# Linear attention with a tree layer: another order of fills, masking on VectorE, low parts on GpSimd

## The reference

```
xn = layernorm(x)
Q = elu(xn @ Wq + bq) + 1;  K = elu(xn @ Wk + bk) + 1;  V = xn @ Wv + bv     # 16 heads of 64
for each token i:  KV += k_i v_i^T;  Ks += k_i
                   o_i = (q_i KV) / (q_i . Ks + 1e-6)
attention = o @ Wo + bo
gate = sigmoid(xn @ Wq2.T @ routers.T)           # 255 nodes of a binary tree of depth 8
leaf = product of the branch probabilities       # 256 leaves
tree = (leaf @ leaf_values) @ Wout.T + Wout_b
out = x + attention + tree
```

## Time and profile before

| | |
|---|---|
| median of three runs | 1221.74 us |
| profiled execution | 1219.74 us, span 1218.0 us |
| PE busy | 1161.8 us, 95% of the span |
| VectorE, ScalarE, GpSimd busy | 836.1, 681.0, 804.3 us |
| granted PE clock, mean | 0.997 of full speed |
| transfers | 84.46 MB in the main queue |

### The profile page before, as it was taken

The page is one execution under the profiler, slowest core; times in us unless marked ns, Lnnn a source line. Parts: engine busy times, 40 slices in busy tenths (PEclk is TensorE's granted clock), DMA queues, the critical chain, the costliest instruction groups (busy, mean ns, idle before and its releaser), DMA issues.

```text
span 1218.0 us, 48108 instructions
## 1 busy us (share of the span) xinstructions
PE 1161.8 (95%) x21233; PEld 996.0 (82%) x21233; DVE 836.1 (69%) x2186; ACT 681.0 (56%) x990; POOL 804.3 (66%) x951
## 2 busy tenths in 40 slices
PE   5899999999999999999999999999999999999986
PEld 4789788887878879778897888878788797888866
DVE  4775875858677585876858667585876758767482
ACT  3563674737557374673737547374673746647371
POOL 3586667667666676766667676676666667676571
PEclk9999999999999999999999999999999999999998
DMA  7143532525344252533524435252452625335251
GB/s 233 20 80 52 86 68 54 91 52 89 60 65 90 45 97 50 89 63 55 93 49 90 58 62 98 45 89 54 84 68 57 94 45 89 63 57 77 55 71 36
DMA packets 271298, 87.54 MB, mean 72 GB/s; under 512 B 250721, under 2 KB 269424, under 8 KB 271088
## 3 DMA queue, kind: packets, MB, share of 16 engines
q1 hardware_dynamic: 271088, 84.46, 39.0%
HBM read 14.43 MB, written 8.39 MB: 19 GB/s over the span
## 4 chain that ended last, share of the span: by engine, by line
PE 63%; DVE 18%; ACT 6%; DMA 5%; issue 4%; POOL 3%; SPq 1%; POOLq 0%; ACTq 0%; DVEq 0%
PE w_pair L811 17%; PE s_pair L811 11%; PE s_pair L826 9%; PE o_pair L826 9%; PE s_pair L893 5%; PE o_pair L947 4%; DVE snaps L732 4%; DVE qT L659 3%; PE o_pair L933 3%; DVE oT L697 3%; DVE v_aug L668 3%; DVE xn L645 2%; DMA k_turned<-k_planes 2%; PE kv_pair L906 2%; ACT ex L522 2%
## 5 line engine op out<-in xcount | busy, mean ns | idle before, releaser
L406 POOL TENSOR_SCALAR_AFFINE_SELECT aT<-aT 64x512 f32<-64x512 f32 x256 | 171.7, 671 | 264.6 <-ACT aT L562 254.9
L562 ACT ACTIVATE aT<-s_pair 128x512 f32<-128x512 f32 x128 | 76.5, 598 | 382.6 <-PE s_pair L893 382.6
L811 PE MATMUL w_pair<-xnT,wk 128*128 128x512 f32 x768 | 212.1, 411 | 2.2 <-ACT k_tok L535 2.2
L811 PE MATMUL s_pair<-xnT,wq 128*128 128x512 f32 x756 | 201.1, 401 | 0.6 <-DVE o_tok L709 0.3
L732 DVE TENSOR_TENSOR snaps<-kv_pair,snaps 128x65 f32<-128x65 f32 x768 | 173.4, 226 | 26.4
L467 POOL COPY k_tok<-k_turned 128x1024 uint16<-128x1024 uint16 x126 | 171.4, 1361 | 22.7 <-POOL ffn_tok L459 14.6
L811 PE MATMUL w_pair<-wv,xnT 128*128 128x512 f32 x654 | 170.0, 395 | 0.0
L525 ACT ACTIVATE ex<-ex 128x512 f32<-128x512 f32 x256 | 161.9, 633 | 8.1
L449 POOL COPY k_planes<-kT 128x1024 uint16<-128x1024 uint16 x126 | 132.7, 1053 | 49.2 <-issue 26.5
L811 PEld LDWEIGHTS w_pair<-xnT,wk 128*128 128x128 f32 x768 | 134.3, 188 | 34.4 <-ACT k_tok L535 2.7
L811 PEld LDWEIGHTS s_pair<-xnT,wq 128*128 128x128 f32 x756 | 135.1, 188 | 27.0 <-DVE o_tok L709 2.4
(11 more groups left out here) (117 smaller groups left out, 2076.6 us busy)
## 6 DMA issues: line engine op xcount, KB each, us to landing
x_in<-in_L_attn_x_dram SPq DMA_DIRECT2D x16, 256.0 KB, 3.1
x_in<-in_L_attn_x_dram SPq DMA_DIRECT2D x32, 128.0 KB, 3.2
out_dram<-y_buf SPq DMA_DIRECT2D x32, 128.0 KB, 1.7
out_dram<-y_buf SPq DMA_DIRECT2D x64, 64.0 KB, 2.3
k_turned<-k_planes SPq DMA_TRANSPOSE x126, 3.2
stage<-in_L_attn_Wv_dram SPq DMA_DIRECT2D x2, 512.0 KB, 7.8
stage<-in_L_attn_Wk_dram SPq DMA_DIRECT2D x2, 512.0 KB, 10.0
stage<-in_L_attn_Wq_dram SPq DMA_DIRECT2D x2, 512.0 KB, 12.2
```

What stands on the lines that cost most here:

```text
L406: pool.affine_select(out=part, in_=part, compare_op=ALU.is_ge, fill=0.0, base=0, pattern=[[0, 2 * CH], [1, D]], channel_multiplier=-1).the ...
L811: last = pe.matmul(dst, l, r, start=i == 0, stop=i == len(steps) - 1)
```

## The change

The order of fills is another. V1(0) of a block moves from unit 0 to unit 7 of the block before, the two transposes of the next input to units 0 and 1, V1(3) to the head of unit 2, and the gate fills become tails of units 2 and 6 (in bank W1). Unit 5 has no head. The masks leave ScalarE and GpSimd: VectorE takes the minimum of the scores and a tile `limit`, which holds the largest float where a score is kept and 0 elsewhere (the scores are not negative). In each unit VectorE does the mask, then the carry, then the normalisation. GpSimd takes the low part of the turned outputs, after its key copies. The residual is added in four parts (units 2 and 6), x is loaded and normalised in unit 7, and the inverse deviation is computed between the tree's levels.

```diff
 def unit_fills(g, p, blocks):
     ...
-    if p == 0:
-        head, tail = [("V1", 0, g)], [("V1", 1, g)]
-    if p in (1, 2):
-        tail = [("V1", p + 1, g)]
-        if more:
-            head = [("xT", p - 1, g + 1)]
-    if p in (3, 4):
-        head = [("leaf", p - 3, g)]
-        if more:
-            tail = [("V0", p - 3, g + 1)]
-    if p in (5, 6) and more:
-        head, tail = [("gate", p - 5, g + 1)], [("V0", p - 3, g + 1)]
+    if g == 0 and p < HALF - 1:
+        head, tail = (([("V1", 0, 0)], [("V1", 1, 0)]), ([("xT", 0, 1)], [("V1", 2, 0)]),
+                      ([("V1", 3, 0)], [("xT", 1, 1)]))[p]
+    elif p < 2:
+        head = [("xT", p, g + 1)] if more else []
+        tail = [("V1", p + 1, g)]
+    elif p == 2:
+        head = [("V1", 3, g)]
+        tail = [("gate", 0, g + 1)] if more else []
+    elif p in (3, 4):
+        head = [("leaf", p - 3, g)]
+        tail = [("V0", p - 3, g + 1)] if more else []
+    elif p == 5 and more:
+        head = [("gate", 0, 1)] if g == 0 else []
+        tail = [("V0", 2, g + 1)]
+    elif p == 6 and more:
+        head, tail = [("V0", 3, g + 1)], [("gate", 1, g + 1)]
+    elif p == PAIRS - 1 and more:
+        head = [("V1", 0, g + 1)]
 ...
 # sync: the load of x
+                if p == PAIRS - 1 and g + 2 < BLOCKS:
+                    sp.wait_ge(x_consumed, CH * (g + 1))
+                    load_block(g + 2)
                 if by_dma(n):
                     turn_output(n)
                 if n + 3 < UNITS:
                     turn_keys(n + 3)
-                if p == 2 and g + 2 < BLOCKS:
-                    sp.wait_ge(x_consumed, g + 1)
-                    load_block(g + 2)
 ...
 # gpsimd
+            pool.memset(limit[:, :], LARGEST).then_inc(limit_step, 1)
+            pool.wait_ge(limit_step, 1)
+            for a in range(2):
+                part = limit[a * D:(a + 1) * D]
+                pool.affine_select(out=part, in_=part, compare_op=ALU.is_ge, fill=0.0, base=0,
+                                   pattern=[[1, D]], channel_multiplier=-1).then_inc(limit_step, 1)
 ...
+            def low_of_turned(n):
+                g, p = divmod(n, PAIRS)
+                pool.wait_ge(oT_hi, n + 1)
+                pool.tensor_tensor(oT[:, 1, p], o_full[:, 1, p], oT[:, 0, p].bitcast(F32), ALU.subtract)\
+                    .then_inc(o_low, 1)
+                pool.wait_ge(o_low, units_by_dma(n))
 ...
             for n in range(UNITS):
                 g, p = divmod(n, PAIRS)
-                if p == 0 and g + 1 < BLOCKS:
-                    inverse_deviation(g + 1)
-                    pool.wait_ge(rstd_ready, 2 * g + 4)
-                if n + 1 < UNITS:
-                    mask(n + 1)
 ...
                 if n + 3 < UNITS:
                     take_apart(n + 3)
-                if p == 1:
-                    residual(g)
-                    pool.wait_ge(x_consumed, g + 1)
+                if n and by_dma(n - 1):
+                    low_of_turned(n - 1)
+                for c in RESIDUAL_AT.get(p, ()):
+                    residual(g, c)
 ...
                     for l in range(depth):
+                        if l == 4 and g + 2 < BLOCKS:
+
+                            inverse_deviation(g + 2)
+                            pool.wait_ge(rstd_ready, 2 * g + 6)
                         level(l, g + 1)
 ...
 # vector
+            def mask(n):
+                dve.wait_ge(s_filled, n + 1)
+                dve.tensor_tensor(aT[:, n % 2],
+                                  s_pair[:, :, 0:CH * D].rearrange("p h (c q) -> p h c q", q=D),
+                                  limit[:, :].unsqueeze(1).unsqueeze(1).to_broadcast([P, 2, CH, D]), ALU.min)\
+                   .then_inc(a_masked, 1)
 ...
             for n in range(UNITS):
                 g, p = divmod(n, PAIRS)
-                norm(n)
+                if n + 1 < UNITS:
+                    mask(n + 1)
                 if n + 1 < UNITS:
                     carry(n + 1)
-                if p == 0 and g + 1 < BLOCKS:
-                    normalise(g + 1)
+                norm(n)
+                if n == 0:
+                    normalise(1)
 ...
                         if p == PAIRS - 1 and g + 2 < BLOCKS:
                             layer_norm(g + 2)
+                            normalise(g + 2)
 ...
 # tensor: waits within and ahead of the fills
+                    if kind == "K":
+                        fill(name, at_last=others_ready)
+                    elif kind == "Q":
+                        fill(name, masked, normed)
+                    else:
+                        fill(name)
```

More of the change, by code:

```diff
@@ L21 @@
 EPS_NORM = 1e-5
+LARGEST = 3.4028234663852886e38
 W0, W1, S0, S1, O0, O1 = range(6)
@@ L145, in attention_and_tree_layer @@
         minus_half = sb("minus_half", [P, CH])
+        limit = sb("limit", [P, D])
         x_in = sb("x_in", [P, 2, CH, hid])
@@ L174, in o_turned @@
         def o_turned(p):
-            place = gate if p < HALF else xn
+            place = gate if p < 2 else xn
             return place[:, 2 * (p % 2):2 * (p % 2) + 2].rearrange("p c n -> p (c n)").bitcast(U16)\
@@ L339, in turn_output @@
                 sp.wait_ge(o_apart, units_by_dma(n))
-                if p == HALF and g + 1 < BLOCKS:
+                if p in (2, 3) and g + 1 < BLOCKS:
                     name = ("xT", 1, g + 1)
@@ L400, in _, with residual @@
             pool.wait_ge(pool_step, 3)
[L402 to L410, removed]
+            def residual(g, c):
                 if g:
@@ L670, in values @@
                    .then_inc(drained[bank_of[name]], 1)
-            def values_first(fills, p):
-                if p not in (2, PAIRS - 2):
-                    return fills
-                return [f for f in fills if f[0] not in ("Q", "V0", "V1", "oT", "kT")] + \
-                    [f for f in fills if f[0] in ("V0", "V1")] + \
-                    [f for f in fills if f[0] in ("Q", "oT", "kT")]
             def low_of_output(name):
@@ L761, in _ @@
             carry(0)
+            dve.wait_ge(limit_step, 3)
+            mask(0)
             phi(("Q", 1, 0))
@@ L766, in _ @@
                 g, p = divmod(n, PAIRS)
-                norm(n)
+                if n + 1 < UNITS:
+                    mask(n + 1)
                 if n + 1 < UNITS:
                     carry(n + 1)
-                if p == 0 and g + 1 < BLOCKS:
-                    normalise(g + 1)
-                fills = [name for name, _ in unit_fills(g, p, BLOCKS)]
-                turned = n and by_dma(n - 1)
-                for name in values_first(fills, p):
+                norm(n)
+                if n == 0:
+                    normalise(1)
+                for name, _ in unit_fills(g, p, BLOCKS):
                     kind, i, b = name
@@ L835, in tile_of_output, with fill @@
                 return slice(at * P, (at + 1) * P)
-            def fill(name, at_last=None):
+            def fill(name, at_half=None, at_last=None):
                 kind, i, g = name
@@ L1052, in normed, with until_inputs, others_ready @@
                     until(o_normed, n + 1)
-                def head_ready():
-                    for kind, i, g in (f for f, _ in fills):
-                        if kind == "xT":
-                            until(xn_ready, g + 1)
-                        if kind == "leaf" and i == 0:
-                            until(leaf_step, (g + 1) * LEVEL_STEPS)
+                def until_inputs(name):
+                    kind, i, g = name
+                    if kind == "xT":
+                        until(xn_ready, g + 1)
+                    if kind == "leaf":
+                        until(leaf_step, (g + 1) * LEVEL_STEPS)
+                    if kind in ("V0", "gate"):
+                        for t in range(KT_):
+                            until_drained(("xT", t, g))
+                def others_ready():
+                    for name, _ in fills:
+                        until_inputs(name)
                 def masked():
                     if n + 1 < UNITS:
-                        until(a_masked, 2 * n + 4)
+                        until(a_masked, n + 2)
                 for name, bank in fills:
@@ L1068, in _ @@
                     if bank in (S0, S1) and n + 1 < UNITS:
-                        until(s_copied, n + 2)
+                        until(a_masked, n + 2)
                     if kind in ("oT", "y"):
                         normed()
-                    if kind == "V0" and i == 0:
-                        for t in range(KT_):
-                            until_drained(("xT", t, g))
-                    if kind == "leaf":
-                        until(leaf_step, (g + 1) * LEVEL_STEPS)
+                    until_inputs(name)
                     if kind == "y" and i == 0:
@@ L1080, in _ @@
                             until_drained(("leaf", t, g))
-                    fill(name, head_ready if kind == "K" else normed if kind == "Q" else masked if bank == W1 and kind in ("V0", "V1") else None)
```

(4 more changed lines are left out.)

45 lines of the change are left out of this document (17 added, 28 removed).

## The result

The changed kernel takes 1257.69 us (median of four runs, 1256.88 to 1258.49) against 1220.23 us before: a ratio of 1.0309, 95% interval 1.0285 to 1.0332. It is slower by 37.5 us. The forecast was 1265, with 1240 to 1285.

A forecast was written before the change was run, and what follows sets the result against it. PE, busy 95%, was taken as the bound; a new loop through k_tok would set units 0 to 6. Middle blocks +37.0, block 0 +2.3, block 15 +4.0, last unit +1: +44.3, about 1265 us, range 1240 to 1285.

The forecast's parts named there:

- The loop: Units 0 to 6: scores, mask, carries, normalisation, POOL's output copy, k_tok, next scores; 7.87 us, 7.62 in a sequence's last block.
- The links: Eight steps of the loop: 0.60, 1.96, 0.44, 0.69, 0.13, 1.11, 1.37 and 1.57 us.
- The point of decision: Loop length in units 0 to 6 below which the kernel would be faster: 7.45 us.
- 7.25 gives 1200: Partial version of the faster rival (1177 us, chance 0.09): a loop of 7.25 us gives 1200 us.
- no change: Rival: loop in units 0 to 6 at 7.42 to 7.48 us leaves the time the same; chance 0.02.
- Unit 7: Last unit of a block: 19.50 plus 1.40 for the V1 fill plus 0.4 for GpSimd's low part, 21.3 us.
- Block 15: Last block: six units from 41.75 us become 6 x 7.62 = 45.7, +4.0 us.
- slower still: Rival: late transposes in 105 units, +21 us, and the clock falling earlier in the last block; about 1290; chance 0.10.
- Block 0: First block, first three units without output by DMA: four units at mean +0.12 and unit 7, about +2.3 us.
- The tail: The last unit gets the slower low part and a later output copy: +1 us.
- Signs: Expected in the profile: PE idle from 56 to about 100 us, o_tok about 3.1 us after the mask, among others.
- The part of the change that gains: Waits in units 0, 2 and 6, some 2.7 us a block; without the loop 1177 us, faster rival, chance 0.09.

The follow-up runs named there:

- Six carries ahead: Changed kernel with VectorE doing six of the eight carries before the normalisation and the others after it; 1220.56 us, ratio 1.0008 against the kernel before.
- the four kernels without the loop: New order of fills, normalisation before carry; mask/low part on GpSimd/VectorE 1179.55, VectorE/VectorE 1177.74, VectorE/GpSimd 1181.93, GpSimd/GpSimd 1194.16 us.
- the order that breaks the loop: Changed kernel with only VectorE's order edited to mask, normalisation, carry; 1181.93 us, ratio 0.9687 against the kernel before.
- the dose: Changed kernel with none, four, six or all eight carries ahead of VectorE's normalisation; 1181.93, 1191.93, 1220.56 and 1257.69 us.
- four carries: Changed kernel with four of the eight carries ahead of VectorE's normalisation and the others behind it; 1191.93 us, ratio 0.9768 against the kernel before.
- a late output: Kernel before with one edit: VectorE does the carry ahead of the normalisation; 1231.35 us, ratio 1.0091.
- a fuller GpSimd: Kernel before with one edit: low parts of the turned outputs on GpSimd, after its key copies; 1233.04 us, ratio 1.0104.

## Why the prediction was right

- *The loop.* It was the step on which the sign rested, and it stands: 7.76 us against 7.87, 7.50 against 7.62 in the last block of a sequence. The links with a row of the same operation were right to 0.02 (carry 1.96, mask to carry 0.60, VectorE to GpSimd 0.13); what was too long is the way from k_tok to the next scores, 1.51 against 1.57 in the earlier trace rows, which comes from a unit with other waits in it, 0.02 each in den and k_tok, and 0.01 in POOL's copy. This is most of what the forecast has too much in blocks 1 to 14: 37.0 forecast, 28.1 measured, 0.11 or 0.12 in each of some 70 units and 0.08 in units 2 and 6.
- *The point of decision*, 7.45 us. Six carries ahead make a loop of 7.25 and 1220.56 us, the time of before, so equality lies lower. My formula let all seven units shrink with the loop, but units 2 and 6 have 7.77 of work: (1028.1 - 298.2)/14 = 52.1 = 5 x 7.32 + 2 x 7.77. With that, 7.32. The same slip is in the rival's "7.25 gives 1200" and in "no change" at 7.42 to 7.48; at 7.25 it was 1220.56.
- *Unit 7*: 21.3 forecast, 21.25 measured; the wait for GpSimd's low part is there, 15 times. With the low part on VectorE it takes 20.9, so the 0.4 for it was 0.3.
- *Block 15*: +4.0 forecast, +4.3 measured. Its unit 3 took 8.10 in place of 7.50, when the granted clock fell, and the unit after it 7.73. The view by stretches has it (from and to, us; then busy us and instructions of PE, PEld, DVE, ACT and POOL; the last three are the granted clock, the DMA share and GB/s):

```profile
1208.00:1212.00 4.00, 2.33 (x101) 2.13 (x104) 1.67 (x3) 1.96 (x5) 3.80 (x4) 0.85 0.37 70
1212.00:1216.00 4.00, 4.00 (x53) 3.38 (x46) 3.15 (x11) 2.04 (x3) 0.83 (x2) 0.73 0.42 66
```

  PE had waited 1.67 us for k_tok just before. In the kernel before the clock stays at 1.0 up to 1192 us, past the end of those six units. The rival "slower still" named this and left some 4 us for it (1290 less 1265 and 21); the two units are 0.8 longer than the loop.
- *Block 0* was mis-sized: +2.3 forecast, +5.4 measured. Its unit 7 is 2.65 longer and not 1.8, for there PE waits 1.1 us for the low part. Its units 3 to 6 are 1.3 longer in all and not 0.5: I had used the mean of whole blocks, in which units 0 and 2 get shorter, where the loop of 7.87 against their 29.8 us gives 1.7. Its units 0, 1 and 2 are 0.2, 0.4 and 0.95 longer, and I had taken them as unchanged. Unit 2 keeps that length with the normalisation first (8.94) and with the order of fills alone (8.96), so it is the new order there.
- *The tail* was to cost 1 and cost nothing (27.6 in both); what lies before block 0 is 0.8 shorter. So the total, 44.3 forecast and 37.0 measured, is closer than its terms: 8.9 too much in the middle and 1.9 at the ends, less 3.4 too little in blocks 0 and 15.
- *Signs.* PE's idle time grew from 56 to 74 us and not to 100; with the 19 us of waits that count as busy in the Q fill it is 93. o_tok starts 2.98 us after the mask; the forecast said 3.1, though its own links add up to 3.00.
- *The part of the change that gains* was named (the stalls of units 0, 2 and 6, 2.7 us a block) and its worth without the loop forecast at 1177; three of the four kernels without the loop take 1178 to 1182, the fourth, with masks and low parts on GpSimd, 1194. Unit 2's stall I laid to the blocked low part. Whether that is its cause stays open. Moving that operation alone did not remove the stall, but put a GpSimd that is late from the residual add in its place. The order of fills removes it with the low part still on VectorE, but splits and moves the residual as well, and there the low part takes at most 1.23 us where it took up to 2.83 before. No kernel changes one of the two alone.

That k_tok waits for o_tok is shown by the order that breaks the loop and by the dose. The late transposes add to it where the loop is just shorter than the work: with four carries, single units wait for k_tok because the key transpose is late.

## What to carry to other kernels

When an operation is moved ahead of another on an engine that has room, follow what waits for the one moved back, from engine to engine, until it comes round to the moved operation's own release. If it does, add the links: a loop longer than the bound engine's work sets the time although the other engines get idler, and one clearly shorter costs nothing; just under the work (6.7 against 6.84 us here) single late transfers still showed. Units of different work that take the same time are its mark.

## What was not expected of the hardware

The transposes on the queue leave little room in the short units: with the normalisation first, POOL waits for the key transpose 36 times, 22.5 us in all and at most 1.0, and with k_tok's copy ahead of the output's single waits became 3.51 and 4.14 us and the units irregular. The median from issue to landing of the key transpose is 3.2 us in the kernel before and 3.6 to 3.8 in all kernels with the new order of fills whose output copy stands first, whether their common unit takes 6.84 or 7.76 us; with the old order and a late output or a fuller GpSimd it is 3.5. So it isn't the length of the units. Why is open.
